# A quarter of the exponentials' sums moved from VectorE to accumulating DMAs, in a fused attention and expert kernel

## The chip, the core and the metric

The kernel runs on one core of a Trainium2 chip. The metric is the device time of one execution in microseconds; lower is better. The core has TensorE (PE, matmuls), VectorE (DVE), ScalarE (ACT), GpSimd (POOL) and SyncE (SP, which here only issues DMAs). On-chip memory is SBUF; matmul results go to PSUM, in eight banks of 128x512 fp32.

## What is computed

The input is x, four images of 64x64 positions with 128 channels, all fp32: four batches of 4096 tokens. For each batch:

```
xn  = group_norm(x)                        # 32 groups
q, k, v = split(xn @ w_qkv)                # 4 heads of 32
q, k    = q / |q|, k / |k|                 # norms over the token axis
a   = softmax(10 * q @ k.T)                # 4096 x 4096 for each head
x   = x + (a @ v) @ w_out + b_out
x   = x + linear_attention(layer_norm(x))  # 4 heads, then a norm over the batch
x   = x + top2_of_8_experts(layer_norm(x))
```

Nearly all the time goes into the softmax attention of the fourth line, and the change is there.

## The kernel before, in words

Each batch has three stages: a preparation (norms, projections, and stacks QS and KS that let one matmul carry the high and low parts of a product), the attention, and the mix (output projection, linear attention, experts). All synchronisation is written by hand: every engine has its own program with waits on counting semaphores, and the order on an engine is the order in the text.

**The attention loop.** Queries are taken in 8 chunks of 512 for a batch (32 chunks in all), and for each chunk keys go by in 32 tiles of 128. A key tile is two *steps*, one for each pair of heads, so a chunk has 64 steps, numbered 0 to 63 here; step 2t+p is pair p of key tile t. For each step PE writes scores (two matmuls, 128x512) into one of three PSUM buffers, and ACT turns them into exponentials (one instruction, 128x1024, line 539) in a ring of 8 slots, E, that lies in the tile KE. For each key tile PE multiplies the exponentials by the values (`values`, four matmuls of 32 output columns for the four heads, each recorded twice in the profile) and accumulates them over the whole chunk in the bank PV.

**PE's order.** `scored_after` and `valued_after` fix it: scores are written three steps at a time, after every third step, and between two such groups come the values of one key tile and of two key tiles by turns. The pattern repeats every six steps, which are three key tiles. Scores of a step wait until ACT has read the buffer that they overwrite.

**The softmax's denominators.** DVE adds the exponentials over key tiles into an accumulator ACC (in the tile XT), one instruction of 128x1024 for each step (line 786). It starts anew in each of five groups of key tiles (`GROUPS`), since the first addition of a group takes two tiles at once: 27 additions for each pair of heads, 54 for a chunk. PE sums each group's accumulator over the 128 keys (`sums`, four matmuls against ones) into the bank SM; the five groups of `sums` for a chunk accumulate there. They come after the values of tiles 8, 14, 20 and 27, and the last one after tile 2 of the next chunk. DVE then takes the reciprocal of SM (`reciprocals`, line 795), ACT copies PV out (`copy_out`, line 523), and POOL multiplies the two (`normalise`, line 432).

**Slots.** An exponential may be written when the values and the addition of the tile four before have been done: ACT waits on `s_pv` and `s_adds` once in two steps.

**Weights.** All weights of all stages are loaded once at the start by SP (line 345) and stay in SBUF; the first x comes after them on the same queue (line 354). SP also loads QS for the next chunk (line 365), the next batch's x when the attention's scores are done, and stores the output (line 388).

The program has a second form of the loop for inputs with large norms (`general`, `safe=False`); with these inputs it does not run.

Of the kernel before, what the change touches and what calls it, by code (L numbers as in the profile page):

```python
# [20 lines left out]
F32 = mybir.dt.float32  # L21
# [7 lines left out]
P = 128  # L29
# [20 lines left out]
RING = 8  # L50

GROUPS = (6, 6, 6, 7, 7)
NG = len(GROUPS)
FIRST = [sum(GROUPS[:g]) for g in range(NG)]
END = [sum(GROUPS[:g + 1]) for g in range(NG)]
ADDS = 2 * (T - NG)
ADDS0 = 2 * (GROUPS[-1] - 1)
LAG = 3
NORMALISED = 5
# [32 lines left out]

def adds_until(j):

    if j < 0:
        return adds_until(T + j) - ADDS
    g = max(g for g in range(NG) if FIRST[g] <= j)
    return 2 * (FIRST[g] - g + max(j - FIRST[g], 1))
# [19 lines left out]
def hybrid_kernel(nc, x, w_qkv0, w_out0, b_out0, w_qkvT, w_outT, b_out1, gn_w, gn_b, router_w, router_b,  # L118
# [5 lines left out]
    with ctx:  # L124
# [26 lines left out]
        E = KE[:, :].rearrange("p (r n) -> p r n", r=RING)  # L151
# [5 lines left out]
        WQKV1 = sb("WQKV1", [P, 3 * C])  # L157
        WOUT1 = sb("WOUT1", [P, C])
        WEXP = sb("WEXP", [P, EXPERTS, C])
# [27 lines left out]
        FLAG = sb("FLAG", [P, 1], I32)  # L187
        PVC = sb("PVC", [P, CH])
# [12 lines left out]
        RM = sb("RM", [P, H, CH], F32, attn)  # L201
        attn.close()
# [3 lines left out]
        XN = sb("XN", [P, T, C], F32, mix)  # L206
        ZX = sb("ZX", [P, 2, 2, NDVE * C], F32, mix)
# [59 lines left out]
        s_adds = sem("s_adds")  # L267
        s_sum = sem("s_sum")
        s_pvc = sem("s_pvc")
# [55 lines left out]

        def stacked(u):

            return KS[:, u % H, u // H * CH:(u // H + 1) * CH]
# [9 lines left out]
        def _(sp):  # L338
            loads = [(WQKV[:, :], w_qkv0), (WOUT0[:, :], w_out0), (WQKV1[:, :], w_qkvT), (WOUT1[:, :], w_outT),
                     (WEXP[:, :, :], expert_w.rearrange("e d c -> d e c")), (WR[:, :], router_w),  # L340
# [41 lines left out]

            def store(b):
                for i in range(4):
                    part = slice(i * T // 4 * C, (i + 1) * T // 4 * C)

                    sp.wait_ge(s_zs, b * PAIRS + (i + 1) * PAIRS // 4)
                    sp.dma_start(out_v[b, :, part], X[:, :, :].rearrange("p t c -> p (t c)")[:, part]).then_inc(s_x_out[i], 16)

            load_x(0)  # L390
            with sp.Fori(0, batches - 1) as b:
                stack(b)

                sp.wait_ge(s_scores, b * SCORED + SCORED)
                load_x(b + 1)
                store(b)
            stack(batches - 1)
            store(batches - 1)
# [4 lines left out]
        def _(pool):  # L403
            pool.sem_inc(s_ot, 1)
            nc.gpsimd.memset(EB[:, :, :], 0.0).then_inc(s_eb0, 1)
            pool.wait_ge(s_const, 12 * 16)
            pool.wait_ge(s_eb, TPB * 16)
            with pool.Fori(0, batches) as b:
# [31 lines left out]

                with pool.If(general):
                    for c in range(2):
                        maxima(c)
                    with pool.Fori(1, NCH) as c:
                        normalise(b * NCH + c, c)
                        maxima(c + 1)
                with pool.Else():
                    pool.sem_inc(s_gred, NCH + 1)
                    with pool.Fori(1, NCH) as c:
                        normalise(b * NCH + c, c)  # L450
# [25 lines left out]
        def _(act):  # L476
            act.sem_inc(s_pvc, 1)
            with act.Fori(0, batches) as b:
# [39 lines left out]
                def copy_out(after):  # L518

                    act.wait_ge(s_pv, after * T + RING // 2)  # L520

# [3 lines left out]
                def exponentials(c, first):  # L525

                    for s in range(STEPS):
# [11 lines left out]
                        nc.scalar.activation(E[:, s % RING, :], S[buffer(s)].rearrange("p a n -> p (a n)"), ACT.Exp,  # L539
# [81 lines left out]
        def _(dve):  # L621
# [51 lines left out]
            dve.sem_inc(s_adds, ADDS0)  # L673
            dve.sem_inc(s_rec, 1)
            dve.sem_inc(s_gmax, 1)
            dve.wait_ge(s_const, 12 * 16)
            with dve.Fori(0, batches) as b:
# [84 lines left out]

                def attend(two, par, safe):
                    c = two * 2 + par
                    chunk = b * NCH + c
                    for g in range(NG):
                        for jt in range(FIRST[g] + 1, END[g]):
                            if jt == NORMALISED:
                                if par:
                                    reciprocals(chunk)  # L770
                                else:
                                    with dve.If(two):
                                        reciprocals(chunk)
                            for p in range(2):
                                acc = ACC[:, (par * NG + g) % 2, p, :]
                                if jt == FIRST[g] + 1:
                                    if p == 0:

                                        dve.wait_ge(s_sum, chunk * NG + g + 1)
                                    one = E[:, (2 * jt - 2 + p) % RING, :]  # L780
                                else:
                                    one = acc

                                    dve.wait_ge(s_adds, chunk * ADDS + ADDS0 + 2 * (jt - g - 1) + p - 1)
                                dve.wait_ge(s_exp, chunk * STEPS + 2 * jt + p + 1)
                                v.tensor_tensor(acc, one, E[:, (2 * jt + p) % RING, :], ALU.add).then_inc(s_adds, 1)  # L786
                    if not safe:
                        maxima(b * GEN + c * STEPS + STEPS)

                def reciprocals(after):  # L790

                    dve.wait_ge(s_sum, after * NG + 2)

                    dve.wait_ge(s_ot, after)
# [571 lines left out]
```

## Time and profile before

| | |
|---|---|
| device time, median of 3 runs | 3317.12 us (3315.71 to 3320.56) |
| the profiled execution's own time | 3316.07 us |
| its span, first to last instruction | 3314.2 us |
| mean granted clock of TensorE | 0.963 of full speed |
| busy: PE, DVE, ACT, POOL | 3082.6, 2877.6, 2438.1, 314.4 us |
| attention of the first batch | from 80 to 654 us of the span |
| mix of the first batch and preparation of the next | from 654 to about 896 us |
| bytes moved by DMA | 56.36 MB, mean 17 GB/s |

The busy times are shares over stages that have different limits, so the table says only that the attention takes some 70% of the time, four stretches like the one from 80 to 654 us. The profile comes from one execution; the medians come from runs without it.

### The profile page before, as it was taken

The page shows a single profiled execution, that of the slowest core. Times are in us where ns is not written, and L with a number is a line of the kernel's source. Part 1 is how long each engine was busy: PE and PEld are TensorE (multiplying, and loading weights), DVE is VectorE, ACT ScalarE, POOL GpSimd, SP SyncE. Part 2 cuts the span into 40 slices and gives each one's busy share as a digit, 9 for nine tenths or more (in the row PEclk, how much of TensorE's full clock was granted, in tenths as well). Part 3 has the DMA queues.
Part 4 walks back from the last instruction along what each step waited for, and adds up shares of the span by engine and source line. Part 5 has one row for each costly group of instructions (what it writes and reads, how often), then busy time and mean ns, then how long its engine had stood idle before and what let it go on. Part 6 is the DMA issues. An engine that isn't in the chain of part 4 may idle for free.

```text
span 3314.2 us, 56981 instructions
## 1 busy us (share of the span) xinstructions
PE 3082.6 (93%) x17608; PEld 1523.2 (46%) x17608; DVE 2877.6 (87%) x3948; ACT 2438.1 (74%) x3308; POOL 314.4 (9%) x281
## 2 busy tenths in 40 slices
PE   6999999979799999998979999999887999999978
PEld 4444343475544434347544444444745444434474
DVE  5899999978799999897879998989787999999977
ACT  5888888744688888874468888887456888888744
POOL 1000000014200000001410000000041000000005
PEclk9999999988899999998989999999898999999989
DMA  2000000000100000000010000000001000000000
GB/s 65 22 14 14 14 14 14 27 1 20 32 16 14 14 14 14 14 27 1 20 34 14 14 14 14 14 14 26 1 20 34 14 14 14 14 17 11 1 1 26
DMA packets 29712, 56.36 MB, mean 17 GB/s; under 512 B 8224, under 2 KB 10304, under 8 KB 28864
## 3 DMA queue, kind: packets, MB, share of 16 engines
q1 hardware_dynamic: 29376, 52.09, 5.5%
q8 instruction: 185, 3.03, 0.4%
q14 instruction: 151, 1.24, 0.1%
HBM read 14.31 MB, written 8.39 MB: 7 GB/s over the span
## 4 chain that ended last, share of the span: by engine, by line
PE 80%; issue 10%; DVE 6%; ACT 2%; POOL 1%; ACTq 0%; SPq 0%; DMA 0%; DVEq 0%; POOLq 0%
PE BK L1005 79%; DVE X L978 2%; PE BK L1010 1%; ACT KE L539 1%; POOL QE L457 1%; DVE ST L686 0%; DVE ST L648 0%; DVE RU L641 0%; DVE KS L735 0%; DVE X L970 0%; ACT BK L494 0%; DVE SMALL L693 0%; DMA XN<-in_x 0%; DVE RU L642 0%; ACT XT L558 0%
## 5 line engine op out<-in xcount | busy, mean ns | idle before, releaser
L539 ACT ACTIVATE KE<-BK 128x1024 f32<-128x1024 f32 x2048 | 1925.8, 1039 | 375.1 <-PE BK L1005 341.6
L786 DVE TENSOR_TENSOR XT<-XT,KE 128x1024 f32<-128x1024 f32 x1408 | 1647.6, 1237 | 9.5 <-ACT KE L539 7.7
L1005 PE MATMUL BK<-QS,KS 128*128 128x512 f32 x4120 | 1209.8, 423 | 53.6 <-ACT KE L539 30.5
L1005 PEld LDWEIGHTS BK<-QS,KS 128*128 128x128 f32 x4120 | 702.2, 190 | 845.8 <-ACT KE L539 727.5
L1005 PE MATMUL BK<-KE,V 128*32 128x512 f32 x8192 | 1026.5, 602 | 0.0
L786 DVE TENSOR_TENSOR XT<-KE 128x1024 f32<-128x1024 f32 x320 | 380.9, 1220 | 194.3 <-ACT KE L539 194.2
L1005 PEld LDWEIGHTS BK<-KE,V 128*32 128x32 f32 x8192 | 194.1, 108 | 447.4 <-issue 352.2
L432 POOL TENSOR_TENSOR QH<-PVC,REC 128x512 f32 (+1 forms) x32 | 62.0, 1939 | 2481.6 <-DVE REC L795 2481.6
L1005 PE MATMUL BK<-WEXP,XT 128*128 128x512 f32 x512 | 236.4, 608 | 15.3 <-DVE X L978 15.3
L616 ACT ACTIVATE ZX<-BK,GT 128x128 f32<-128x128 f32 x512 | 146.3, 368 | 131.4 <-PE BK L1005 131.4
L978 DVE SCALAR_TENSOR_TENSOR X<-BK,GT,X 128x128 f32<-128x128 f32 x512 | 175.2, 350 | 31.6 <-PE BK L1005 15.1
L553 ACT ACTIVATE QL<-X,NM,RY 128x128 f32<-128x128 f32 x128 | 51.0, 481 | 170.9 <-DVE NM L665 170.9
L1005 PE MATMUL BK<-XT,CONST 128*32 128x512 f32 x1280 | 166.7, 592 | 0.0
L1005 PEld LDWEIGHTS BK<-WEXP,XT 128*128 128x128 f32 x512 | 95.0, 195 | 123.0 <-issue 102.4
L1005 PE MATMUL BK<-XT,WQKV 128*128 128x512 f32 x192 | 97.8, 664 | 14.8 <-DVE XT L702 14.8
L466 POOL TENSOR_TENSOR Z<-ZX 128x512 f32<-128x512 f32 x64 | 81.1, 1267 | 294.4 <-ACT ZX L616 294.4
L795 DVE RECIPROCAL REC<-BK 128x512 f32<-128x512 f32 x32 | 107.2, 3351 | 0.0
L1005 PEld LDWEIGHTS BK<-WQKV,XT 128*128 128x128 f32 x768 | 87.7, 192 | 3.8 <-issue 3.8
L1005 PE MATMUL BK<-WQKV,XT 128*128 128x128 f32 x768 | 88.4, 275 | 0.0
L1005 PEld LDWEIGHTS BK<-XT,CONST 128*32 128x32 f32 x1280 | 41.2, 110 | 93.8 <-issue 73.6
L1010 PE MATMUL BK<-CONST,QL 128*128 128x128 f32 x256 | 52.1, 379 | 33.0 <-DVE QL L668 30.8
L1005 PE MATMUL BK<-AT,QT 128*128 128x128 f32 x512 | 68.8, 303 | 14.5 <-DVE AT L903 14.5
(151 smaller groups left out, 1834.0 us busy)
## 6 DMA issues: line engine op xcount, KB each, us to landing
QS<-QP SPq DMA_DIRECT2D x448, 64.0 KB, 2.0
XN<-in_x SPq DMA_DIRECT2D x16, 512.0 KB, 6.0
out<-X SPq DMA_DIRECT2D x16, 512.0 KB, 2.6
QSF<-in_consts SPq DMA_DIRECT2D x4, 1024.0 KB, 4.9
WEXP<-in_L_ffn_expert_w SPq DMA_DIRECT2D x1, 512.0 KB, 3.9
CONST<-in_consts SPq DMA_DIRECT2D x1, 384.0 KB, 10.0
WQKV<-in_L_conv_w_qkv SPq DMA_DIRECT2D x1, 192.0 KB, 2.3
WQKV<-in_L_attn_W_qkv SPq DMA_DIRECT2D x1, 192.0 KB, 3.0
```

Of the source, the lines that this page charges most:

```text
L432: nc.gpsimd.tensor_tensor(QH[:, bass.ts(place, CH)], PVC[:, :], REC[:, :], ALU.mult).then_inc(s_ot, 1)
L457: nc.gpsimd.tensor_tensor(q, q, r, ALU.mult).then_inc(s_q1n, 1)
L466: nc.gpsimd.tensor_tensor(Z2[:, :, :], z[:, :, 0:2 * C], z[:, :, 2 * C:4 * C], ALU.add).then_inc(s_zs, 1)
L539: nc.scalar.activation(E[:, s % RING, :], S[buffer(s)].rearrange("p a n -> p (a n)"), ACT.Exp, scale=SCALE0).then_inc(s_exp, 1)
L553: last = nc.scalar.activation(QL[:, t * C:(t + 1) * C], X[:, t, :], ACT.Identity, bias=NM[:, t:t + 1], scale=RY[:, t:t + 1])
L616: last = nc.scalar.activation(ZX[:, t // 2 % 2, t % 2, k], expert_bank(t, 1)[:, k], ACT.Copy, scale=GT[:, t, e:e + 1])
L786: v.tensor_tensor(acc, one, E[:, (2 * jt + p) % RING, :], ALU.add).then_inc(s_adds, 1)
L795: v.reciprocal(REC[:, :], SM).then_inc(s_rec, 1)
L978: v.scalar_tensor_tensor(X[:, t, :], expert_bank(t, 0)[:, e * C:(e + 1) * C], GT[:, t, e:e + 1], X[:, t, :], ALU.mult, ALU.add).then_inc(s ...
L1005: return nc.tensor.matmul(o, lhsT, rhs, start=start, stop=stop, skip_group_check=shared)
L1010: last = nc.tensor.transpose(dst[:, (t % TPB) * P:(t % TPB + 1) * P], src(t), IDENT)
```

## The change

Three things are changed together.

1. **Where exponentials are kept and added.** Key tiles 1, 5, 9, ... 29 (`aside`: eight of 32) get a buffer of their own, EA, with room for one tile (both pairs of heads). The other 24 use a ring of four tiles in KE. Tiles 5 to 29 in EA are added by seven DMAs for a chunk that accumulate (`accum_op=ALU.add`) from EA to DACC in SBUF, 128 rows of 8 KB each. POOL issues each when both exponentials are there, waits until it has landed, and then raises `s_free`; ACT waits for that before it writes the next tile into EA. Tile 1 is added by DVE: DACC is started as tile 1 plus tile 3, and tiles 0 and 2 start ACC. DVE adds the 21 other tiles to ACC, and adds DACC of the chunk before to its ACC (`merge`) just after tiles 0 and 2 of the next chunk. The last chunk's `merge` stands in the mix, after the second addition of the projection to X.
2. **One group of `sums` for a chunk** in place of five, after the values of tile 4 of the next chunk; `reciprocals` comes before tile 8's addition in place of tile 5's.
3. **Weights of the mix** (WQKV1, WOUT1, WEXP) share the attention's space and are loaded for each batch by SP, when the scores are done, ahead of the next batch's x. PE waits for them before the mix's transposes. At the start three loads fall away.

The core of the diff (the form for large norms, which changes too, is left out):

```diff
-RING = 8
-GROUPS = (6, 6, 6, 7, 7)
...
-LAG = 3
-NORMALISED = 5
+RING = 4
+HEAD = 6
+def aside(jt):
+    return jt % 4 == 1
+ASIDE = T // 4
+ADDED = [jt for jt in range(T) if not aside(jt) and jt > 3]
+ADDS = 2 * (2 + len(ADDED))
+DADDS = ASIDE - 1
+SUMMED = 4
+NORMALISED = 8
+def slot(jt):
+    return (jt - (jt + 2) // 4) % RING
+def held_before(jt):
+    return max(w for w in range(jt - 8, jt) if not aside(w % T) and slot(w % T) == slot(jt))
...
+        EA = sb("EA", [P, 2, 2 * CH], F32, attn)
+        DACC = RM[:, :, :].rearrange("p (s i) n -> p s (i n)", s=2)
...
+            def load_weights():
+                sp.dma_start(WQKV1[:, :], w_qkvT).then_inc(s_w1, 16)
+                sp.dma_start(WOUT1[:, :], w_outT).then_inc(s_w1, 16)
+                sp.dma_start(WEXP[:, :, :], expert_w.rearrange("e d c -> d e c")).then_inc(s_w1, 16)
...
                 sp.wait_ge(s_scores, b * SCORED + SCORED)
+                load_weights()
                 load_x(b + 1)
...
+                def accumulate(c, k):
+                    chunk = b * NCH + c
+                    jt = 4 * k + 1
+                    pool.wait_ge(s_exp, chunk * STEPS + 2 * jt + 2)
+                    settle(pool)
...
+                    nc.gpsimd.dma_start(DACC, EA[:, :, :], accum_op=ALU.add).then_inc(s_dacc, 16)
+                    freed(c, k)
+                def freed(c, k):
+                    pool.wait_ge(s_dacc, (b * NCH + c) * (16 * DADDS) + 16 * k)
+                    pool.sem_inc(s_free, 1)
...
+                    with pool.Fori(0, NCH) as c:
+                        for k in range(1, ASIDE):
+                            if k == 4:
+                                with pool.If(c):
+                                    normalise(b * NCH + c, c)
+                            accumulate(c, k)
...
-                            act.wait_ge(s_pv, b * (NCH * T) + c * T + jt + 1)
-                            act.wait_ge(s_adds, b * (NCH * ADDS) + c * ADDS + ADDS0 + adds_until(jt - RING // 2))
+                            before = jt - 4 if aside(jt) else held_before(jt)
+                            act.wait_ge(s_pv, chunk * T + (HEAD + before + 1))
+                            if jt == 1:
+                                act.wait_ge(s_free, chunk * DADDS + 1)
+                            elif aside(jt) and jt > 5:
+                                act.wait_ge(s_free, chunk * DADDS + jt // 4)
+                            else:
+                                act.wait_ge(s_adds, chunk * ADDS + (ADDS0 + adds_until(before)))
...
+                    for p in range(2):
+                        dve.wait_ge(s_exp, chunk * STEPS + 2 * 2 + p + 1)
+                        v.tensor_tensor(ACC[:, par, p, :], exps(0, p), exps(2, p), ALU.add).then_inc(s_adds, 1)
+                    before(lambda: merge(chunk, 1 - par, safe))
...
+                    for p in range(2):
+                        dve.wait_ge(s_exp, chunk * STEPS + 2 * 3 + p + 1)
+                        if safe:
+                            dve.wait_ge(s_merge, chunk * 2 + (MERGE0 + p - 1))
+                            v.tensor_tensor(DACC[:, p, :], exps(1, p), exps(3, p), ALU.add).then_inc(s_adds, 1)
...
-                            if jt == LAG - 1:
+                            if jt == SUMMED:
                                 if par:
-                                    sums(NG - 1, chunk * ADDS + ADDS0, 0)
+                                    sums(chunk, 0)
...
-                            for g in range(NG - 1):
-                                if jt == END[g] - 1 + LAG:
...
-                                    sums(g, chunk * ADDS + (ADDS0 + 2 * (END[g] - g - 1)), par)
...
+                        if c == 1 and ready is s_y0:
+                            dve.wait_ge(s_zero, b + 1)
+                            merge(b * NCH + NCH, 1, True)
...
+                pe.wait_ge(s_w1, b * 48 + 48)
```

## Rows read from the trace of the kernel before

**Rows 1.** Busy time in stretches: two chunks of attention, then a mix.

```profile
core 0: us, PE busy (x) PEld busy (x) DVE busy (x) ACT busy (x) POOL busy (x), PEclk, DMA share, GB/s
...
224.00:367.50 143.50, 141.23 (x848) 57.79 (x848) 132.17 (x110) 121.23 (x131) 4.07 (x2) 1.00 0.07 16
...
655.00:838.00 183.00, 154.39 (x801) 112.58 (x800) 144.63 (x452) 83.83 (x222) 51.48 (x55) 0.90 0.05 20
```

**Rows 2.** Chain that ended last, the first loop pair (start us, us, what).

```profile
223.37 1.03 ACT KE L539
...
224.79 70.62 PE BK L1005 x424
...
366.89 1.03 ACT KE L539
```

**Rows 3.** ACT's timeline: start, us, instructions, [idle before <-releaser].

```profile
368.27 6.54 ACT L539 ACTIVATE KE<-BK 128x1024 f32<-128x1024 f32 x7
376.27 5.61 ACT L539 ACTIVATE KE<-BK 128x1024 f32<-128x1024 f32 x6 [1.46 <-PE BK L1005]
...
389.52 5.60 ACT L539 ACTIVATE KE<-BK 128x1024 f32<-128x1024 f32 x6 [0.99 <-PE BK L1005]
395.73 5.61 ACT L539 ACTIVATE KE<-BK 128x1024 f32<-128x1024 f32 x6 [0.60 <-PE BK L1005]
402.78 5.60 ACT L539 ACTIVATE KE<-BK 128x1024 f32<-128x1024 f32 x6 [1.45 <-PE BK L1005]
...
422.24 5.61 ACT L539 ACTIVATE KE<-BK 128x1024 f32<-128x1024 f32 x6 [0.60 <-PE BK L1005]
428.44 2.85 ACT L539 ACTIVATE KE<-BK 128x1024 f32<-128x1024 f32 x3 [0.59 <-PE BK L1005]
431.88 2.86 ACT L539 ACTIVATE KE<-BK 128x1024 f32<-128x1024 f32 x3 [0.59 <-PE BK L1005]
435.33 1.94 ACT L539 ACTIVATE KE<-BK 128x1024 f32<-128x1024 f32 x2 [0.59 <-PE BK L1005]
...
439.45 6.52 ACT L539 ACTIVATE KE<-BK 128x1024 f32<-128x1024 f32 x7
```

**Rows 4.** DVE's timeline in the same chunk.

```profile
369.34 2.36 DVE L786 TENSOR_TENSOR XT<-KE 128x1024 f32<-128x1024 f32 x2 [3.79 <-ACT KE L539]
371.62 6.93 DVE L786 TENSOR_TENSOR XT<-XT,KE 128x1024 f32<-128x1024 f32 x6
378.47 3.35 DVE L795 RECIPROCAL REC<-BK 128x512 f32<-128x512 f32 x1
```

**Rows 5.** The end of the attention and the start of the mix, all engines.

```profile
652.83 1.92 SPq L354 DMA_DIRECT2D XN<-in_x  x4
...
655.65 0.69 DVE L818 TENSOR_TENSOR X<-BK,X 128x512 f32<-128x512 f32 x1 [0.20 <-PE BK L1005]
...
665.22 3.68 PE L1010 MATMUL BK<-CONST,QL 128*128 128x128 f32 x16 [3.95 <-DVE QL L668]
```

**Rows 6.** The start of the run: SP's loads, PE's first work.

```profile
2.60 0.43 SPq L345 DMA_DIRECT2D WEXP<-in_L_ffn_expert_w  x1
...
17.44 6.10 PE L1010 MATMUL BK<-CONST,XN 128*128 128x128 f32 x32 [17.44 <-DMA XN<-in_x]
```

**Rows 7.** The page's DMA issues: kind, KB each, median us to landing.

```profile
QS<-QP SPq DMA_DIRECT2D x448, 64.0 KB, 2.0
...
out<-X SPq DMA_DIRECT2D x16, 512.0 KB, 2.6
...
WEXP<-in_L_ffn_expert_w SPq DMA_DIRECT2D x1, 512.0 KB, 3.9
```

**Rows 8.** The last store alone: timeline, to SP's issue.

```profile
3310.34 0.72 POOL L473 TENSOR_TENSOR X<-X,Z 128x256 f32<-128x256 f32 x1
3311.09 0.33 SPq L388 DMA_DIRECT2D out<-X  x1
```

**Rows 9.** The microsecond in which that store moves (columns as rows 1).

```profile
3312.00:3313.00 1.00, 0.00 (x0) 0.00 (x0) 0.00 (x0) 0.00 (x0) 0.00 (x0) 0.50 1.00 410
```

More of the change, by code:

```diff
@@ L49 @@
 SCORED = STEPS * NCH + AHEAD
-RING = 8
-GROUPS = (6, 6, 6, 7, 7)
[L53 to L57, printed above, removed]
-LAG = 3
-NORMALISED = 5
+RING = 4
[5 more added lines that the diff above has]
+ADDS = 2 * (2 + len(ADDED))
+ADDS0 = 10
+DADDS = ASIDE - 1
+MERGE0 = 2
+SUMMED = 4
+NORMALISED = 8
 QLOADS = (NCH + 1) * 16 * 4 * H
@@ L96, in adds_until @@
         return adds_until(T + j) - ADDS
-    g = max(g for g in range(NG) if FIRST[g] <= j)
-    return 2 * (FIRST[g] - g + max(j - FIRST[g], 1))
+    return 2 if j in (0, 2) else 4 if j in (1, 3) else 2 * (3 + ADDED.index(j))
 HALF = T // 2
@@ L187, in hybrid_kernel @@
         FLAG = sb("FLAG", [P, 1], I32)
+        NIL = sb("NIL", [P, 2, 1])
         PVC = sb("PVC", [P, CH])
@@ L448, in _ @@
                     pool.sem_inc(s_gred, NCH + 1)
-                    with pool.Fori(1, NCH) as c:
-                        normalise(b * NCH + c, c)
+                    with pool.Fori(0, NCH) as c:
+                        for k in range(1, ASIDE):
+                            if k == 4:
+                                with pool.If(c):
+                                    normalise(b * NCH + c, c)
+                            accumulate(c, k)
                 normalise(b * NCH + NCH, 0)
@@ L765, in attend @@
                     chunk = b * NCH + c
[L766 to L786, printed above, removed]
@@ new lines, in before, with direct @@
+                    def before(work):
+                        if par:
+                            work()
+                        else:
+                            with dve.If(two):
+                                work()
+                    def direct(jt):
+                        for p in range(2):
+                            acc = ACC[:, par, p, :]
+                            dve.wait_ge(s_exp, chunk * STEPS + 2 * jt + p + 1)
+                            dve.wait_ge(s_adds, chunk * ADDS + (ADDS0 + adds_until(jt - 1) + p - 1))
+                            v.tensor_tensor(acc, acc, exps(jt, p), ALU.add).then_inc(s_gadd, 1)
@@ new lines, in attend @@
+                    for i, jt in enumerate(ADDED):
+                        if jt == NORMALISED:
+                            before(lambda: reciprocals(chunk))
+                        if not safe and aside(jt - 1):
+                            direct(jt - 1)
+                        for p in range(2):
+                            acc = ACC[:, par, p, :]
+                            dve.wait_ge(s_exp, chunk * STEPS + 2 * jt + p + 1)
+                            if not safe and aside(jt - 1):
+                                dve.wait_ge(s_gadd, chunk * (2 * ASIDE) + 2 * (jt // 4) + p + 1)
+                            dve.wait_ge(s_adds, chunk * ADDS + (ADDS0 + 2 * (2 + i) + p - 1))
+                            v.tensor_tensor(acc, acc, exps(jt, p), ALU.add).then_inc(s_adds, 1)
@@ L1199, in _ @@
                 project(3)
-                sums(NG - 1, (b * NCH + NCH) * ADDS + ADDS0, 1)
+                sums(b * NCH + NCH, 1)
                 project(4)
```

97 lines of the change are left out of this document (68 added, 29 removed).

## The prediction, made before the changed kernel ran

> **What bounds the kernel now.** I first read busy time by stretches [rows 1]: over 143.5 us, two chunks, PE is busy for 141.2, DVE for 132.2, ACT for 121.2. Then the chain of waits [rows 2]: the first chunk after a loop-back is one run of 424 PE instructions, 70.62 us long, and a pair of chunks takes 366.89 - 223.37 = 143.52 us, 71.76 a chunk. Then ACT's timeline [rows 3], which shows the beat. ACT does six exponentials in 5.61 us (0.92 apart, 1.03 long), idles 0.6 us on PE, and starts again after 6.21 us (389.52 to 395.73). Where a group of `sums` lies between, the beat is 7.05 (395.73 to 402.78). So PE sets the pace, ACT has 0.6 us in 6.2 to spare, and one group of `sums` costs 0.85 us. The one after tile 27 falls into the other half of the beat: 422.24 to 428.44 to 435.33 is 6.20 and then 6.89, so it costs 0.69. DVE's additions stand 1.14 us apart (six in 6.93, each 1.23) [rows 4].
>
> **The change part by part.** The sum is made against the profiled execution, 3316.07 us (its span of 3314.2 and 1.9 around it); the median is 1.05 above it.
>
> *Sums.* Five groups become one: the cost goes from 4 x 0.85 + 0.69 = 4.09 to 0.85 us, so -3.24 us a chunk. The one left waits for `merge`, which comes before tile 4's values in DVE's order (below); I charge no wait.
>
> *DVE.* 54 additions become 48 (23 tiles or pairs and one merge, twice). That is 48 x 1.14 + 3.35 for the reciprocal [rows 4] = 58 us, under any pace here; DVE was not the bound, so this gives nothing by itself. Its order costs something, though. Before, the first addition starts when step 2 is there (369.34). Now the first needs step 4, which ends at 368.27 + 2 x 0.92 + 1.03 = 371.14 [rows 3]. Six additions follow: tiles 0 and 2, merge, tiles 1 and 3. The sixth ends at 371.18 + 5 x 1.14 + 1.23 = 378.11. Exponential 10 writes tile 5 over tile 1 in EA and waits for just that addition. Without the `sums` that stood ahead of it, ACT would reach it at 376.27 - 0.85 + 0.92 = 376.34 [rows 3]. Behind it on ACT are all later exponentials, and PE's next scores wait for steps 10 and 11: +1.8 us a chunk. Bounds: nothing, if PE is late itself; 1.8.
>
> *The larger ring.* Tiles outside EA get five tiles' distance in place of four. ACT's idle time in these rows ends with PE's scores [rows 3], so a longer reach gives nothing.
>
> *The last merge.* It stands in DVE's run from 655.65 to the normalised tiles, for which PE waits 3.95 us [rows 5]: 2 x 1.14 = 2.3 us on the path, four times, +9.2 us.
>
> *Weights.* At the start three issues of 0.43 us, with 0.04 between, go from SP's queue ahead of x, for which PE waits until 17.44 [rows 6]: -1.4 us (bounds 0 and -4, as 0.7 MB less goes ahead of x). Later they go out at 652.83, ahead of x of the next batch, and the largest takes 3.9 us [rows 7]; PE comes to its wait at 665.22 - 3.95 = 661.3 [rows 5], so they are covered. Uncovered they would cost some 4 us a batch. The next x starts 1.4 us later and is needed only in the next batch's preparation, some 130 us on.
>
> Without the DMAs' part: 32 x (-3.24 + 1.8) + 9.2 - 1.4 = **-38 us**.
>
> *The accumulating DMAs.* EA holds one tile, so the exponentials of steps 8k+2 wait until the DMA for steps 8k-6 and 8k-5 has landed. Call L the time from the end of such a tile's second exponential to the start of the next tile's first. A turn is then L + 0.92 + 1.03 = L + 1.95 us. Six such turns lead from step 10 to step 58. At PE's beat these 48 steps take 8 x 6.2 + 0.85 = 50.45 us, which leaves 6.46 for L. The turn over the chunk's end has 8.1 us (431.88 - 0.6 to 439.45 [rows 3]) and is covered. So the DMAs cost 6 x (L - 6.46) a chunk, 192 x (L - 6.46) us in all, when L is above 6.46, and nothing below. All parts together are neutral at L = 6.46 + 38/192 = **6.66 us**. This number decides.
>
> No row shows such a DMA, nor one issued by POOL. The nearest is the last store, which runs alone: 512 KB, from SBUF, in long rows, lands 2.6 us after its issue [rows 7], and for one microsecond all 16 engines are busy at 410 GB/s [rows 8, 9]. Its data take 1.3 us, so 1.3 are fixed. A copy of 1 MB would take 1.3 + 2.56 = 3.9. But an addition must bring in source and destination, 2 MB: 1.3 + 5.1 = 6.4. Four hand-offs between engines lie on the way (ACT, POOL, DMA, POOL, ACT), 0.03 to 0.04 us each [rows 8] (POOL's end at 3311.06, SP's issue at 3311.09), and POOL builds the descriptors itself, for which I allow 0.5 us, my least founded figure. L = 6.4 + 0.2 + 0.5 = **7.1 us**. The bounds: one pass at full speed with the hand-offs, 4.1 us, no stall; and two passes at the pace of the QS loads, which are SBUF to SBUF and move 16 GB/s with a share of 0.07 [rows 1], 229 GB/s at a full share: 9.2 + 1.3 + 0.7 = 11.2 us. I take 7.1 since the rows are 8 KB long here, more like the store's 4 KB than QS's 2 KB.
>
> That an addition costs a second reading is what the Trainium skill says too ("Collectives: The Full Stack", the section on the bandwidth ceiling: a reducing transfer puts two reads on one ring and gets half a copy's rate, 32 against 62 GB/s there). The skill's fit for a GpSimd DMA ("DMA: Bandwidth & Descriptors", anatomy of the SWDGE path), 2.0 us plus bytes at 436 GB/s, would give 4.4 us for one pass and 6.8 for two, which with the hand-offs is an estimate of 7.0. No run here shows either.
>
> POOL's `normalise` (2.0 us) stands ahead of the fourth DMA, in the 1.95 us in which the tile's exponentials are made, so it delays it by 0.1 us at most.
>
> Sum: -38 + 192 x 0.64 = -38 + 123 = **+85 us**, 3401 for the profiled execution, 3402 for the median.
>
> **The rivals.**
> A, the other side: the addition goes at a copy's pace or is otherwise under 6.46 us, with L from 4.1. Then ACT never waits for EA, the 3.24 us of `sums` are the gain and the result is 3317 - 38 = 3279. For it: DMA engines are nearly idle (share 0.07 [rows 1]), and what a DMA adds may stay inside one pass. Against it: the doubled reading. It decides below L = 6.66; within 0.034 us of that (0.2% is 6.6 us, about what a measurement of this kernel can tell from no change) the result is "same".
> B: adding is slower than reading, L near 11.2. Then 192 x 4.74 = +910 us, and the turn over the chunk's end is too long as well, by 11.2 - 8.1 = 3.1 us, up to 32 x 3.1 = +99: about 4290. For it: the QS loads' pace.
> C: the first turn's stall is absent (DVE's order does not matter), 58 us less in any case: with A it makes 3221.
> Between my case and B, L = 8.4 gives 3317 - 38 + 372 = 3651.
>
> **How the numbers follow.** L between 6.7 and 8.4, my case: 0.45; L above 8.4, B and what lies before it: 0.15; within 0.2% of before: 0.04; A: 0.33, and with C 0.03 more. So faster 0.36, same 0.04, slower 0.60. The likeliest case gives 3402, with its own range from 3325 to 3650. Since cases of both signs hold much, the range reaches from 3265 (A, with a little more from the start of the run) to 3650: 0.15 is left above and about 0.03 below.
>
> **What would show it.** A beat without `sums` of 6.2 us between ACT's groups. Exponential 10 idle for 1.8 us on DVE. Exponentials 18, 26, 34, 42, 50 and 58 idle on POOL or the DMA, with turns of 9.05 us (A: 8.3, B: 13). The DMA's time to landing in the list of issues, near 6.7 us. DVE's idle time up by some 7 us a chunk. PE's clock still 1.00 in the attention; should it drop as PE idles, every number gets worse. The prediction is wrong if the time to landing is under 6 us, or over 8.

## The result, and the profile after

The changed kernel takes 3653.77 us (median of four runs, 3644.67 to 3658.83). The kernel before, on the same chip, takes 3318.28 (3315.71 to 3320.56). The ratio is 1.1008 [1.0981, 1.1036]: 10% slower. The forecast was 3402; its own range (3325 to 3650) and the wide one (to 3650) both end just under the result. The direction was right, and so was the wait that was named for it (ACT's wait for EA); the size was not: +337 us instead of +85. What the wait is made of was sized too low, and one turn that was called covered is not.

The page of the changed kernel, first the chain that ended last, then the costliest groups and the list of DMA issues (kind, KB each, median us to landing):

```profile
span 3656.9 us, 55560 instructions
...
PE 3152.3 (86%) x16584; PEld 1506.7 (41%) x16584; DVE 2642.2 (72%) x3756; ACT 2444.9 (67%) x3308; POOL 493.4 (13%) x506
...
DMA 30%; PE 29%; issue 20%; ACT 11%; DVE 8%; ACTq 1%; POOL 1%; POOLq 0%; DVEq 0%; SPq 0%
...
L616 ACT ACTIVATE EA<-BK 128x1024 f32<-128x1024 f32 x512 | 497.1, 1025 | 390.4 <-POOLq L495 327.9
L489 POOL DMA_DIRECT2D RM<-EA x224 | 194.0, 866 | 2358.7 <-ACT EA L616 1688.7
...
RM<-EA POOLq DMA_DIRECT2D x224, 1024.0 KB, 7.0
```

PE no longer sets the end: DMA has 30% of the chain, and ACT sat idle 327.9 us ahead of the exponentials that write EA until POOL raised `s_free`. The rows that answer to [rows 3], ACT's timeline in a chunk after a loop-back (start, us, instructions, [idle before <-releaser]):

```profile
438.91 1.94 ACT L616 ACTIVATE EA<-BK 128x1024 f32<-128x1024 f32 x2 [4.40 <-POOLq L495]
...
448.62 1.94 ACT L616 ACTIVATE EA<-BK 128x1024 f32<-128x1024 f32 x2 [0.18 <-POOLq L495]
...
458.27 1.94 ACT L616 ACTIVATE EA<-BK 128x1024 f32<-128x1024 f32 x2 [1.49 <-POOLq L495]
460.10 5.62 ACT L616 ACTIVATE KE<-BK 128x1024 f32<-128x1024 f32 x6
467.85 1.94 ACT L616 ACTIVATE EA<-BK 128x1024 f32<-128x1024 f32 x2 [2.14 <-POOLq L495]
```

Each pair of exponentials into EA waits for POOL, and what ACT does between them, six exponentials, no longer fills the time. A regular turn is 458.27 - 448.62 = 9.65 us or 467.85 - 458.27 = 9.58, where PE's beat asked for 8.3. The turn before them is longer. The chain of waits says what each is made of (start, us, what):

```profile
427.99 1.03 ACT EA L616
429.06 0.50 issue
429.58 9.18 DMA RM<-EA
...
439.83 1.03 ACT EA L616
...
440.90 0.59 issue
...
441.51 6.96 DMA RM<-EA
448.47 0.02 issue
448.50 0.03 POOLq L495
...
448.54 0.04 ACTq L615
...
448.62 0.05 ACT EA L616
```

From the end of the exponential (440.86) to the start of POOL's issue are 0.65 us (0.59 of them on POOL itself, between its wait and the issue), from there to the landing 6.96, and 0.15 lead to ACT's next. The turn ahead had a landing time of 9.18.

Over all 192 such turns of the trace (six in each of 32 chunks) the mean is 0.66 + 7.31 + 0.19 = 8.16 us from the end of a tile's second exponential to the start of the next tile's first. This is the L of the forecast, 7.1 there.

### The profile page after: what moved, and what is told of

It is laid out like the page before. It is cut to its first block, busy times and chain, and to the rows that moved or that the text cites. A ratio compares the mean times of both kernels' runs of the same rounds, so it can differ in the third digit from the quotient of the medians.

```text
span 3656.9 us, 55560 instructions
## 1 busy us (share of the span) xinstructions
PE 3152.3 (86%) x16584; PEld 1506.7 (41%) x16584; DVE 2642.2 (72%) x3756; ACT 2444.9 (67%) x3308; POOL 493.4 (13%) x506
## 4 chain that ended last, share of the span: by engine, by line
DMA 30%; PE 29%; issue 20%; ACT 11%; DVE 8%; ACTq 1%; POOL 1%; POOLq 0%; DVEq 0%; SPq 0%
DMA RM<-EA 29%; PE BK L1128 28%; ACT EA L616 7%; ACT KE L616 3%; DVE XT L908 2%; DVE X L1101 2%; PE BK L1133 1%; POOL QE L527 1%; ACTq L615 1%; DVE RM L893 0%; DVE ST L764 0%; DVE ST L725 0%; DVE RU L718 0%; DVE KS L813 0%; DVE X L1093 0%
## 5 line engine op out<-in xcount | busy, mean ns | idle before, releaser
L908 DVE TENSOR_TENSOR XT<-XT,KE 128x1024 f32<-128x1024 f32 x1344 | 1556.8, 1219 | 570.8 <-ACT KE L616 570.4
L616 ACT ACTIVATE KE<-BK 128x1024 f32<-128x1024 f32 x1536 | 1467.9, 1047 | 307.9 <-PE BK L1128 289.9
L1128 PE MATMUL BK<-QS,KS 128*128 128x512 f32 x4120 | 1325.3, 442 | 321.9 <-ACT EA L616 259.2
L1128 PE MATMUL BK<-KE,V 128*32 128x512 f32 x6144 | 826.3, 626 | 0.0
L616 ACT ACTIVATE EA<-BK 128x1024 f32<-128x1024 f32 x512 | 497.1, 1025 | 390.4 <-POOLq L495 327.9
L489 POOL DMA_DIRECT2D RM<-EA x224 | 194.0, 866 | 2358.7 <-ACT EA L616 1688.7
L1128 PEld LDWEIGHTS BK<-KE,V 128*32 128x32 f32 x6144 | 145.3, 110 | 340.4 <-issue 284.8
L1128 PE MATMUL BK<-EA,V 128*32 128x512 f32 x2048 | 285.2, 630 | 0.0
L882 DVE TENSOR_TENSOR XT<-KE 128x1024 f32<-128x1024 f32 x64 | 75.6, 1222 | 206.9 <-ACT KE L616 206.9
L1101 DVE SCALAR_TENSOR_TENSOR X<-BK,GT,X 128x128 f32<-128x128 f32 x512 | 175.8, 350 | 33.6 <-PE BK L1128 17.4
L1128 PEld LDWEIGHTS BK<-EA,V 128*32 128x32 f32 x2048 | 53.2, 114 | 131.6 <-issue 86.7
```

The lines of the kernel that those rows point to most:

```text
L489: nc.gpsimd.dma_start(DACC, EA[:, :, :], accum_op=ALU.add).then_inc(s_dacc, 16)
L616: nc.scalar.activation(exps(jt, p), S[buffer(s)].rearrange("p a n -> p (a n)"), ACT.Exp, scale=SCALE0).then_inc(s_exp, 1)
L882: v.tensor_tensor(ACC[:, par, p, :], exps(0, p), exps(2, p), ALU.add).then_inc(s_adds, 1)
L908: v.tensor_tensor(acc, acc, exps(jt, p), ALU.add).then_inc(s_adds, 1)
L1101: v.scalar_tensor_tensor(X[:, t, :], expert_bank(t, 0)[:, e * C:(e + 1) * C], GT[:, t, e:e + 1], X[:, t, :], ALU.mult, ALU.add).then_inc(s ...
L1128: return nc.tensor.matmul(o, lhsT, rhs, start=start, stop=stop, skip_group_check=shared)
```

## The stages, measured in every run

In each trace I took the time from a batch's first exponential to its last (attention), and the gaps between batches. The last column is what follows the last exponential; all in us. Each row is one trace, and a batch or a gap differs from its neighbours in the same trace by up to 4 us.

| kernel | first exponential | attention, four batches | three gaps | end |
|---|---|---|---|---|
| before | 79.98 | 571.1, 570.9, 573.9, 572.9 | 251.7, 252.1, 251.7 | 190.0 |
| changed | 74.69 | 654.8, 655.2, 651.6, 657.2 | 253.4, 256.2, 256.2 | 197.5 |
| DMAs left out (e1) | 74.41 | 560.9, 562.2, 561.0, 561.1 | 254.6, 254.1, 258.0 | 197.6 |
| also no merge (e8) | 74.38 | 546.3, 546.3, 546.1, 546.9 | 255.6, 252.8, 256.0 | 195.5 |
| weights alone (e6) | 73.94 | 570.9, 570.7, 573.0, 571.2 | 251.7, 255.6, 252.7 | 191.7 |
| two slots (e5) | 73.95 | 558.7, 561.0, 559.4, 559.5 | 256.2, 255.0, 256.4 | 196.4 |
| four tiles (e4) | 73.51 | 564.7, 550.2, 549.6, 550.2 | 257.8, 258.5, 259.0 | 199.1 |
| four tiles again (e10) | 74.86 | 550.3, 549.2, 550.5, 565.1 | 256.0, 259.3, 258.4 | 198.2 |
| four tiles, merge first (e9) | 74.28 | 550.3, 550.7, 550.8, 549.3 | 258.7, 258.0, 257.9 | 199.4 |
| copy (e2) | 73.55 | 564.9, 564.0, 562.7, 561.5 | 257.7, 255.0, 253.4 | 194.2 |
| half the bytes (e3) | 74.30 | 563.1, 562.5, 564.5, 565.1 | 256.3, 253.6, 257.5 | 197.7 |
| one group of sums (e7) | 80.13 | 593.3, 593.1, 593.0, 592.9 | 257.5, 256.5, 257.6 | 193.2 |

## The experiments

### The change without its DMAs (e1_no_dma)

POOL raises `s_free` without starting a DMA, so the exponentials of seven tiles of a chunk (5, 9 ... 29) are missing from the sums. The rest of the change stays.

```diff
-                    nc.gpsimd.dma_start(DACC, EA[:, :, :], accum_op=ALU.add).then_inc(s_dacc, 16)
-                    freed(c, k)
+                    pool.sem_inc(s_free, 1)
```

> The changed kernel with the seven accumulating DMAs of a chunk left out: POOL raises s_free at once when both exponentials of the tile are there, so tiles 5, 9 ... 29 are missing from the denominators. Everything else stays: DVE's order, the single group of sums, the weights loaded for each batch. Theory W (what costs the time is ACT's wait for the one-tile buffer, 7.65 us from the end of a tile's second exponential to the next tile's first): the rest of the change is worth what was worked out before, -38 us, so 3265 to 3295. Rival R (the rest of the change costs it: the later first addition, the one group of sums, the merge in the mix): 3400 or more. Rival T (traffic: the DMAs slow the engines or the code loads): like W here, told apart from it by the two-slot and four-tile kernels.

Measured: 3288.62 us, ratio 0.9913 [0.9897, 0.993]. The other parts gain some 30 us, and the DMAs alone cost 365. ACT's timeline shows both terms of the forecast for a chunk:

```profile
433.55 1.03 ACT L615 ACTIVATE KE<-BK 128x1024 f32<-128x1024 f32 x1 [0.59 <-PE BK L1127]
436.34 1.94 ACT L615 ACTIVATE EA<-BK 128x1024 f32<-128x1024 f32 x2 [1.77 <-DVE RM L892]
...
442.48 2.86 ACT L615 ACTIVATE KE<-BK 128x1024 f32<-128x1024 f32 x3 [1.45 <-PE BK L1127]
445.21 1.96 ACT L615 ACTIVATE EA<-BK 128x1024 f32<-128x1024 f32 x2
447.01 1.07 ACT L615 ACTIVATE KE<-BK 128x1024 f32<-128x1024 f32 x1
448.69 4.69 ACT L615 ACTIVATE KE<-BK 128x1024 f32<-128x1024 f32 x5 [0.60 <-PE BK L1127]
453.23 1.07 ACT L615 ACTIVATE EA<-BK 128x1024 f32<-128x1024 f32 x1
454.89 1.03 ACT L615 ACTIVATE EA<-BK 128x1024 f32<-128x1024 f32 x1 [0.60 <-PE BK L1127]
```

Exponential 10 stands idle 1.77 us for DVE, the group of `sums` shows as the one idle time of 1.45, and after it the beat is PE's, 442.48 to 448.69 to 454.89, 6.2 us with 0.6 idle: no wait on POOL is left. The attention became shorter by 10.9 us a batch (571.1, 570.9, 573.9, 572.9 to 560.9, 562.2, 561.0, 561.1), 1.36 a chunk where 1.44 was forecast.

### The price of exponential 10's wait, and of the last merge (e8_no_dma_no_merge)

In e1, DVE's two merging additions a chunk are left out as well, so the sums also lack tiles 1 and 3.

```diff
-                    for p in range(2):
-                        acc = ACC[:, par, p, :]
-                        dve.wait_ge(s_adds, chunk * ADDS + (ADDS0 + p - 1))
-                        v.tensor_tensor(acc, acc, DACC[:, p, :], ALU.add).then_inc(s_merge, 1)
+                    dve.wait_ge(s_adds, chunk * ADDS + ADDS0)
+                    dve.sem_inc(s_merge, 2)
```

> The kernel without the accumulating DMAs, and without the merge too (DACC is added nowhere, so tiles 1 and 3 are missing from the denominators as well). With two additions less ahead of it, the one that exponential 10 waits for ends at 375.8 in the prediction's count, before 376.3. Theory: 1.8 us a chunk and 2.3 us a batch go: 3288.6 - 57 - 9 = 3223 (3215 to 3232). Rival C of the prediction (PE is late there itself and DVE's order costs nothing): 3279 to 3289.

Measured: 3222.33 us, ratio 0.9713 [0.9698, 0.9728]. Beside e1 the attention is 59.6 us shorter over the four batches, 1.86 a chunk, where 1.8 was forecast: the stall is real and costs its full length, and rival C falls. Against the kernel before, the attention is 103 us shorter, 3.23 a chunk: the forecast's saving on `sums` (3.24), alone. The gaps and the end became shorter by 4.4 us in all, 1.1 a batch; the forecast took 2.3 a batch for the merge. In e1's trace the merge does stand in DVE's run between two additions to X and lasts as long as forecast (DVE's timeline):

```profile
3091.45 2.35 DVE L850 TENSOR_TENSOR XT<-XT,RM 128x1024 f32<-128x1024 f32 x2
```

At most about half of its 2.35 us reaches the end, and how much is not settled: gaps and end are 960 us in e8 and 964 in e1, but also 960 in e2, which has the merge.

### One pass in place of two: a copy, and half the bytes (e2_copy, e3_half)

In e2 (the first added line) the DMA copies EA over RM and adds nothing, so that only the last tile set aside reaches the sums, and tiles 1 and 3 are lost too. In e3 (the second) it adds only the first half of the tile, 512 KB, and leaves the other half out.

```diff
-                    nc.gpsimd.dma_start(DACC, EA[:, :, :], accum_op=ALU.add).then_inc(s_dacc, 16)
+                    nc.gpsimd.dma_start(DACC, EA[:, :, :]).then_inc(s_dacc, 16)
+                    nc.gpsimd.dma_start(DACC[:, 0:1, :], EA[:, 0:1, :], accum_op=ALU.add).then_inc(s_dacc, 16)
```

> The changed kernel with the same seven DMAs issued by POOL, but as plain copies from EA to DACC, without the addition (so the denominators are wrong). Theory W2 (an addition reads source and destination, so its data take two passes, 4.9 us, and 2.1 us are fixed): time to landing 4.4 to 4.9 us in place of 7.0, which is below the 6.46 us that ACT leaves, so 3270 to 3310 us. Rival F (a DMA issued by POOL has a high fixed cost and the addition costs nothing): landing 6.5 to 7.0 and 3600 to 3650 us.

> The changed kernel, but each accumulating DMA adds only the first pair of heads' 512 KB of the tile (the other pair's exponentials of tiles 5 to 29 are missing from the denominators). Theory W2 (2.1 us fixed, and two passes over the data): the data part halves, landing 2.1 + 2.45 = 4.6 us, no wait on ACT, 3280 to 3300 us. Rival F (fixed cost, or a cost for each of the 128 rows, which stay 128): landing 6 us or more, above 3400.

Measured, one run each: 3289.04 and 3296.39 us. Both are near e1's 3288.62: a DMA that lands in 4.5 or 4.6 us costs next to nothing (the attention is 2 to 3 us a batch longer than e1's), although it is issued as often and writes as many bytes (e2) or is as much an addition (e3). The landing times of the three kernels (the view of RM's tile; us, smallest, median, largest), changed kernel, e2, e3:

```profile
DMA to landing us min/median/max: 6.9/7.0/9.2
```

```profile
DMA to landing us min/median/max: 4.3/4.6/6.6
```

```profile
DMA to landing us min/median/max: 4.5/4.5/6.2
```

So an addition of 1 MB takes 2.4 us longer than a copy of 1 MB, and twice the bytes of an addition take 2.5 us longer than half of them. That is what a second pass over the bytes, as the forecast charged it, would take; no view shows the reading itself. The Trainium skill ("Collectives: The Full Stack", the section on the bandwidth ceiling) says that a reducing transfer reads twice and so gets half of a copy's rate, and the 2.4 us fit this. Its fit for a GpSimd DMA ("DMA: Bandwidth & Descriptors", anatomy of the SWDGE path), 2.0 us plus bytes at 436 GB/s, gives as an estimate 4.4 us for one pass and 6.8 for two, against the measured 4.6 and 7.0.

### A second slot (e5_two_slots)

All the work is kept. Tiles 5, 13, 21 and 29 are written to the second half of X, so a slot has two turns' time for its DMA (and the output is wrong, since X is overwritten). The edit takes away a second wait as well: exponential 10 now writes to X and no longer waits for DVE's addition of tile 1.

```diff
+        EX = X[:, T // 2:T, :].rearrange("p t c -> p (t c)").rearrange("p (s n) -> p s n", s=2)
...
-            return EA[:, p, :] if aside(jt) else E[:, slot(jt), p, :]
+            return (EA if jt % 8 == 1 else EX)[:, p, :] if aside(jt) else E[:, slot(jt), p, :]
...
-                    nc.gpsimd.dma_start(DACC, EA[:, :, :], accum_op=ALU.add).then_inc(s_dacc, 16)
+                    nc.gpsimd.dma_start(DACC, EX if k % 2 else EA[:, :, :], accum_op=ALU.add).then_inc(s_dacc, 16)
...
-                            elif aside(jt) and jt > 5:
+                            elif jt == 5:
+                                act.wait_ge(s_free, chunk * DADDS + 2)
+                            elif aside(jt) and jt > 9:
                                 act.wait_ge(s_free, chunk * DADDS + jt // 4)
```

> The changed kernel with a second slot for tiles set aside, used by turns with EA (it lies over half of X, so the residual input is overwritten and the output is not the reference's). All seven DMAs of a chunk stay, one after the other. Theory W: a landing may take up to 6 to 8 tiles' time, so neither the 7.65 us nor the late landings of 9.3 us are waited for: 3265 to 3310 us. Rival T: the traffic is the same as in the changed kernel, so much of the 337 us stays, 3450 or more. Rival R: 3400 or more.

Measured: 3279.06 us, ratio 0.9888 [0.9866, 0.9909]. The 224 additions are as long as before (6.9 to 9.8 us, median 7.0). ACT's waits for POOL are gone, and the six turns of a chunk from tile 5 to tile 29 take 50.3 us, as in e8, where they took 60.6: so the wait on the one slot is what made the turns long, and neither the traffic nor the issues on POOL.

Something of the DMAs' cost is left all the same, though e5 is 10 us under e1. Exponential 10 does not wait (ACT's timeline, where e1 has 1.77 us of idle time):

```profile
366.00 1.94 ACT L619 ACTIVATE X<-BK 128x1024 f32<-128x1024 f32 x2
```

That alone is worth the 59.6 us between e1 and e8. The fair comparison is with e8, which has neither wait and no DMA: e5's attention is 53 us longer over the four batches, and its median 57 us. The extra time lies around the 12 loop-backs between chunks of a batch: from tile 29's first exponential to exponential 10 of the next chunk are 23.7 us against 19.2 in e8, and without a loop-back 17.4 in both. The merge, which e8 lacks, explains little of it: e4 and e10 have it, have no wait either, and take 19.5. What happens at the loop-back is shown further down. So rival T falls at its price, but some 50 us of it are real.

### The weights alone (e6_weights_alone)

The kernel before, with `w_qkvT`, `w_outT` and `expert_w` taken out of the first loads and loaded for each batch, as in the change.

```diff
+            def load_weights():
+                sp.dma_start(WQKV1[:, :], w_qkvT).then_inc(s_w1, 16)
+                sp.dma_start(WOUT1[:, :], w_outT).then_inc(s_w1, 16)
+                sp.dma_start(WEXP[:, :, :], expert_w.rearrange("e d c -> d e c")).then_inc(s_w1, 16)
...
+                load_weights()
                 load_x(b + 1)
...
+                pe.wait_ge(s_w1, b * 48 + 48)
```

> The kernel before with the weights' part of the change alone (loaded for each batch, three loads less at the start). The kernel without DMAs began its exponentials 5.6 us earlier, and took 3.8 us more between the batches and 7.6 us more after the last, where the merge should cost 2.3. Theory: the start is the weights' part alone, and their loads cost nothing later: -5 us, 3311 to 3315. Rival: the loads delay the mix and take the rest of those sums, 1.5 us three times and 5 us at the end: 3318 to 3324.

Measured: 3314.95 us, ratio 0.999 [0.9981, 0.9999]. PE's first work, which answers to [rows 6], starts earlier by 4.8 us (PE's timeline):

```profile
12.62 5.47 PE L1018 MATMUL BK<-CONST,XN 128*128 128x128 f32 x32 [12.62 <-DMA XN<-in_x]
```

The first exponential comes 6.0 us earlier; some 6 us go back in the gaps (4.5 in all) and the end (1.7), so that little is left. The time is the theory's, but these 6 us are in part what the rival said.

### One group of sums without DMAs (e7_one_group)

The kernel before with all 32 tiles in one group. DVE then adds 31 pairs a chunk instead of 27.

```diff
-GROUPS = (6, 6, 6, 7, 7)
+GROUPS = (32,)
...
                     pe.wait_ge(s_adds, adds)
+                    if NG == 1:
+                        pe.wait_ge(s_rec, s_rec_needed)
```

> The kernel before with one group of sums for a chunk and nothing else: no tile set aside, no DMA, so DVE adds 31 times for each pair of heads, 62 a chunk. Theory: 62 x 1.14 + 3.35 = 74.0 us of DVE work for a chunk, over PE's 68.5, so DVE becomes the bound: 3317 + 32 x 2.3 = 3391 (3370 to 3430). Rival (PE still sets the pace, and DVE's work was never near it): 3317 - 104 = 3213 to 3240.

Measured: 3417.56 us, ratio 1.0294 [1.0279, 1.031]. DVE is now the bound (stretch of two chunks, columns as [rows 1]):

```profile
383.00:526.00 143.00, 134.77 (x744) 50.44 (x740) 143.00 (x121) 117.83 (x123) 4.07 (x2) 1.00 0.05 12
```

The 3.24 us of `sums` can't be had by grouping alone: something has to take four pairs of additions from DVE.

### Half as many tiles by DMA (e4_four_tiles, e10_four_again)

The whole computation is kept. Only tiles 1, 9, 17 and 25 go aside: three DMAs a chunk, 56 additions on DVE, and a turn of eight tiles, 16.5 us at PE's beat. `normalise` stands ahead of the second DMA.

```diff
+ASIDES = (1, 9, 17, 25)
...
-    return jt % 4 == 1
+    return jt in ASIDES
...
-                    jt = 4 * k + 1
+                    jt = ASIDES[k]
...
-                            if k == 4:
+                            if k == 2:
```

> The changed kernel with four key tiles of 32 set aside (1, 9, 17, 25), so three DMAs a chunk and 56 additions on DVE in place of 48. Theory W: a turn of eight key tiles is 16.5 us, far over 9.6, and exponential 10 waits for no addition any more, so PE's beat decides: 71.76 - 3.24 = 68.5 us a chunk, 3317 - 104 + 8 = 3221; DVE has 56 x 1.14 + 3.35 = 67.2 us of work for it, so anything it loses at the chunks' starts shows, 3215 to 3270. Rival R: above 3330, since sums, order and merge stay. Rival T: three sevenths of the extra time stay, 3317 + 0.43 x 337 = 3460.

Measured: 3257.53 us, ratio 0.9809 [0.9786, 0.9831], and the same kernel once more:

> The four-tile kernel once more, on the same chip as the one with the merge first, for their difference. 3252 to 3263; the difference to the other is 9 us by the theory, nothing by the rival.

Measured: 3255.47 us, ratio 0.9809 [0.9795, 0.9824]. This beats both kernels, by 1.9% and by 11%. Exponential 10 now writes tile 5 into the ring and no longer waits, so the chunk has the 3.24 of `sums` without the 1.8: 550.0 / 8 = 68.8 us in three of the batches. The remaining one took some 15 us more (the first, 564.7, in e4; the last, 565.1, in e10; none in e9). It is one chunk of 82.7 us, in which POOL's `normalise`, ahead of the second DMA, took 28.15 us (28.11 in e10) where the median is 1.8. ACT waited for the DMA behind it:

```profile
241.22 28.15 POOL L474 TENSOR_TENSOR QH<-PVC,REC 128x512 f32 x1 [7.21 <-DMA RM<-EA]
...
276.42 1.94 ACT L620 ACTIVATE EA<-BK 128x1024 f32<-128x1024 f32 x2 [13.11 <-POOLq L498]
```

No accumulating DMA was in flight then, and DVE was busy for the whole of its first 13.8 us; why `normalise` became so long no run shows. DVE is close to its limit in a stretch of two chunks, and twice ACT waits for it (ACT's timeline):

```profile
383.00:526.00 143.00, 140.46 (x816) 57.95 (x820) 139.99 (x117) 125.65 (x137) 10.01 (x9) 1.00 0.29 61
```

```profile
464.90 1.94 ACT L620 ACTIVATE KE<-BK 128x1024 f32<-128x1024 f32 x2 [0.67 <-DVE XT L912]
467.17 1.94 ACT L620 ACTIVATE KE<-BK 128x1024 f32<-128x1024 f32 x2 [0.33 <-DVE XT L912]
```

### The last merge ahead of the additions to X (e9_merge_first)

Taken from e4; the whole computation is kept.

```diff
-                        onto_x(ready, done, c)
-                        if c == 1 and ready is s_y0:
+                        if c == 0 and ready is s_y0:
                             dve.wait_ge(s_zero, b + 1)
                             merge(b * NCH + NCH, 1, True)
+                        onto_x(ready, done, c)
```

> The four-tile kernel with the last chunk's merge ahead of the first addition to X in place of behind the second. DVE idles 2.3 us there for PE's first projection, so the two additions of 1.14 us should fit. Theory: 2.3 us a batch come back, 3257.5 - 9 = 3248 (3240 to 3254). Rival: the additions are late there themselves (the last tile's additions end after ACT's last exponential) and push the first addition to X back as they pushed the third: 3255 to 3262.

Measured: 3265.89 us, ratio 0.9853 [0.9825, 0.988], with runs from 3251.61 to 3285.17 and one of 5142.56 that nothing explains (the ratio leaves it out). There is no gain to be told: gaps and end together are 974.0 us here, 971.9 in e10 and 974.4 in e4. DVE's timeline says why:

```profile
619.87 10.29 DVE L912 TENSOR_TENSOR XT<-XT,KE 128x1024 f32<-128x1024 f32 x9
630.09 2.34 DVE L855 TENSOR_TENSOR XT<-XT,RM 128x1024 f32<-128x1024 f32 x2
```

With 56 additions a chunk DVE comes to the merge straight from its additions, without idle time, and the additions to X stand behind it. The 2.3 us of the expectation are DVE's idle time at this place in e1 (2.29), with 48 additions; e4's own trace has none there. In e1 the merge might fit. That was not tried.

## Why the prediction was off, point by point

The step that failed is the term L (7.1 us) with what hung on it: the hand-offs and the landing were sized too low, and "the turn over the chunk's end has 8.1 us and is covered" was wrong. The profiled executions differ by 3656.9 - 3314.2 = 342.7 us, where the sum had 85. By its steps:

- **The parts without the DMAs: -38 forecast, -30 measured (e1).** Attention -43.6 for -46.1. The start -5.6 for -1.4: taking three loads from ahead of x is worth more than their issues, and my bound of -4 was too near. The gaps and the end +18.8 for +9.2. Of that the weights take 6.2 (e6) where I had called them covered, and the merge some 4 (e8) in place of 9.2; some 8 us there stay open. The errors nearly cancel, which is luck.
- **The break-even: L = 6.66 us forecast.** It holds within what was tried: at 4.5 and 4.6 us of landing next to nothing is lost (e2, e3), at 7.0 much is.
- **The hand-offs: 0.2 us forecast, 0.85 measured.** The time from issue to landing was well forecast at its typical value, 6.4 and 0.5 for the descriptors against 7.0. For the hand-offs I took four of 0.03 to 0.04 us from a hand-off of POOL to SP. Measured are 0.66 us ahead of the issue and 0.19 behind the landing, and 0.59 of the first lie on POOL itself. The regular turns of 9.65 and 9.58 us mean L = 7.65. At the forecast's own rate that is 192 x (7.65 - 6.46) = 228 us, for 123.
- **The regular turn is not the mean one.** Over all chunks the six turns from tile 5 to tile 29 take 60.60 us on the mean, where e1 takes 50.75 (forecast 50.45): +9.85 a chunk, 315 in all, of which 87 are not in the 228. One turn at a fixed L is all the forecast had, and the mean L is 8.16. Most of the difference is the landing itself: its mean over the 192 turns is 7.31 us for a median of 6.96, which is 68 us, and 25 of these landings take over 8.5 us, like the 9.18 shown. The first turn of a chunk waits 0.3 us more for POOL's issue, 10 us in all.
- **"The turn over the chunk's end has 8.1 us and is covered."** It failed. The 8.1 were read from the kernel before and still held the 0.69 us of the `sums` after tile 27, which the change itself takes away. In e1 the turn from an even chunk to an odd one takes 9.38 us, so its room is 9.38 - 1.95 = 7.43, enough for 7.1 but less than the L that came; in the changed kernel it takes 10.36, and in nine of the 16 ACT waits for POOL there: 16 x 0.98 = 16 us. From odd to even, over the loop-back, e1 takes 10.50 and the changed kernel 13.67, 12 x 3.17 = 38 us. None of it is a wait for tile 1's slot: 1.86 us of the 3.17 are ACT's longer idle time at the loop-back, 22 us in all, for which the forecast had no term; the other 1.3 are exponential 62's longer wait for PE, behind the last slow turn.
- **Right:** the stall of exponential 10 (1.77 for 1.8, and e8 shows that it costs what it lasts), the saving on `sums` (e8), PE's beat of 6.2 us, the length of a landing as of two passes, and DVE not being the bound. That the larger ring is worth nothing fits the sums of e1 and e8; no run tried it alone.

The sum of the misses: 8 for the other parts, 228 - 123 = 105 for the hand-offs, 315 - 228 = 87 for the longer turns, and 373 - 315 = 58 for the chunks' ends and what little is left, together 258 = 343 - 85. Here 373 is the attention of the changed kernel less that of e1. That the 315 and the 16 at the even chunks' ends come from the wait on the one slot is shown by e5, which has all the DMAs and takes no longer there than e8. The longer idle time at the loop-backs stays in e5 and is longer still.

## What to carry to other kernels

A wait once per turn on one buffer costs its excess every time: work out the whole loop (hand-offs, issue, transfer, release) against the beat, with the spread of the transfer and not only its median, and where the margin is under a few tenths of a microsecond, take a second buffer or make the turn longer first. Here a landing of 4.6 us was nearly free and one of 7.0 cost 365 us; with two slots the same DMAs cost the turns nothing and some 50 us at the loop-backs. Four tiles were spared those, since no addition is in flight when ACT jumps back; that is worth a look wherever a loop goes with long transfers. And when an experiment takes one wait away, look whether it took another with it: e5's total alone would have hidden those 50 us. When work goes to DMA queues, look also at what the new order makes the old engines wait for: half as many tiles by DMA was the better split, because it also took away the 1.8 us on DVE.

## What the runs showed of the hardware that I had not expected

**POOL's way to a DMA.** The issue of a 1 MB addition takes POOL 0.86 us, that of a 1 MB copy 0.53 (e2). From what it waits for to the start of the issue are about 0.6 us.

**Late landings go with code loads.** Around the 9.18 us landing of above (429.58 to 438.76) the DMA view of 436 to 439 us shows one packet of an instruction queue beside the last 16 of the addition:

```profile
q8 instruction: 1, 0.02, 1.9%
q0 software_dynamic: 16, 0.00, 0.8%
```

On the chain of waits are 143 landings, and 28 of them took over 8.5 us instead of 7.0. In the last part of the landing (from 4 us after the issue) all 28 late ones have a packet of queue q8; of 103 that took under 7.6 us, 21 have one, and 20 more have one of the other instruction queue, q14, alone, which no late one has. So it goes with lateness but does not always bring it, and no run took the packets away: whether it is the cause stays open. Copies have late ones too (up to 6.6 for 4.6).

**At a loop-back ACT's idle time follows an instruction packet, which is late under the additions.** At the loop-back ACT is idle without a releaser. In the chain of waits of the kernel before, of the changed one, and of the one with two slots:

```profile
219.58 2.40 issue
...
363.08 2.41 issue
```

```profile
233.48 3.91 issue
```

```profile
348.64 5.98 issue
```

Without the DMAs (e1) it is 2.4 to 2.5. Narrow windows of the DMA view find the packet of instruction queue q14 that goes with it: in the kernel before at 363.96 us, just as ACT's last exponential of the chunk ends (363.99), and with two slots at 352.99, 3.4 us after that end (349.56); windows 363.9 to 364.0 and 352.9 to 353.1:

```profile
q14 instruction: 1, 0.01, 23.9%
```

```profile
q14 instruction: 1, 0.01, 9.8%
```

Each trace has 12 loop-backs within the batches. At every one of them, in nine traces, ACT's next exponential starts 1.9 to 2.2 us after that packet. The packet comes within 0.25 us of the last exponential in the five without an accumulating DMA in flight there (before, e1, e8, e4, e10), up to 0.5 us after it with copies, 0.4 to 0.6 with half the bytes, 1.3 to 3.1 in the changed kernel, and 2.3 to 3.5 in ten of the 12 with two slots (in the other two it is on time, and ACT idles 4.3 to 4.5 us three exponentials later). ACT's idle time there is 1.9 to 2.0 us on the mean without an addition in flight, 3.8 in the changed kernel and 5.3 in those ten. So the idle time grows by as much as the packet is late, and the packet is late only with the DMAs in flight; e4, whose last DMA of a chunk has landed by then, is spared. That ACT waits for this packet is the plain reading; no run moved the packet alone.

**TensorE's clock.** In the attention of the changed kernel the granted clock is 0.95 over 167 us, and for some microseconds it falls to the lower of its levels, 1.2 GHz (columns as [rows 1]):

```profile
240.00:407.00 167.00, 146.54 (x785) 57.37 (x786) 117.22 (x98) 121.89 (x132) 15.48 (x16) 0.95 0.49 102
...
408.00:410.00 2.00, 1.96 (x6) 0.70 (x10) 0.14 (x1) 2.00 (x3) 0.00 (x0) 0.50 0.29 69
```

PE's timeline shows what it did before: it idled 3.18 us and then 2.16, and each time a run of 8 matmuls soon takes 1.95 us instead of 1.07.

```profile
394.31 0.74 PE L1128 MATMUL BK<-QS,KS 128*128 128x512 f32 x2 [3.18 <-ACT EA L616]
...
397.31 1.95 PE L1128 MATMUL BK<-EA,V 128*32 128x512 f32 x8
...
402.62 1.07 PE L1128 MATMUL BK<-KE,V 128*32 128x512 f32 x8
405.84 2.01 PE L1128 MATMUL BK<-QS,KS 128*128 128x512 f32 x4 [2.16 <-ACT KE L616]
...
409.19 1.94 PE L1128 MATMUL BK<-KE,V 128*32 128x512 f32 x8
```

In [rows 1] the two chunks before had 1.00. This slows the matmuls behind a late slot, but it is not what the longer turns above are made of: those end with POOL's release, at a mean of 0.19 us after the landing for a median of 0.15, so at most some 7 us over the 192 turns can be anything else's.
